# Computing the routed experts of a decoder layer on the chosen rows only, through device memory, instead of every expert on every row

## The reference

```python
x = x + attn(layernorm(x), Wqkv, Wo)            # causal, 16 heads of 16
x = x + xattn(layernorm(x), ctx, mask)          # one head of 256, softmax over 256 context rows
x = x + ffn(layernorm(x), ...)

def ffn(x):                                     # 1024 rows of 256
    probs = softmax(xf @ gate_w.T)              # 8 experts
    topk_p, topk_i = top_k(probs, 2)
    comb = (one_hot(topk_i, 8) * topk_p[..., None]).sum(axis=1)
    h = silu(einsum('nc,eic->eni', xf, w1)) * einsum('nc,eic->eni', xf, w2)    # i = 176
    y = einsum('enc,ne->nc', einsum('eni,eci->enc', h, w3), comb)
    sh = silu(xf @ sw1.T) * (xf @ sw2.T) @ sw3.T                               # width 352
    return y + sh
```

## Time and profile before

| | |
|---|---|
| median of 3 runs | 270.72 us |
| profiled execution, its span | 271.7 us |
| PE busy | 259.4 us, 95% |
| ACT busy | 174.8 us, 64% |
| DVE busy | 170.0 us, 63% |
| POOL busy | 122.4 us, 45% |
| bytes moved by DMA | 17.08 MB |

### The profile page before, as it was taken

How to read it: one execution, slowest core, us unless ns; L and a number is a source line. 1 busy time by engine, 2 the same in 40 slices (tenths; PEclk the granted TensorE clock), 3 DMA queues, 4 the chain that set the end, 5 groups by cost and what they waited for, 6 DMA issues and landing times.

```text
span 271.7 us, 4900 instructions
## 1 busy us (share of the span) xinstructions
PE 259.4 (95%) x1805; PEld 210.2 (77%) x1810; DVE 170.0 (63%) x361; ACT 174.8 (64%) x292; POOL 122.4 (45%) x133
## 2 busy tenths in 40 slices
PE   7888989999999999999989999999999999999994
PEld 2447756768877787868778888888989898888884
DVE  3675886867778666776852579638446634545453
ACT  7479379889967799888888855627565313222230
POOL 4447454988776918990954780334320000000000
PEclk9997999999999999999999999999999999999999
DMA  7891000000000000006609600000000079000002
GB/s 235 328 397 70 1 5 2 0 5 0 2 0 0 5 0 4 1 5 229 195 12 249 170 0 4 2 0 2 0 0 2 14 230 255 6 0 4 0 0 78
DMA packets 11879, 17.08 MB, mean 63 GB/s; under 512 B 1904, under 2 KB 8272, under 8 KB 11856
## 3 DMA queue, kind: packets, MB, share of 16 engines
q1 hardware_dynamic: 11856, 16.78, 19.6%
HBM read 15.63 MB, written 1.08 MB: 62 GB/s over the span
## 4 chain that ended last, share of the span: by engine, by line
PE 71%; POOL 8%; DMA 6%; DVE 6%; issue 4%; ACT 3%; SPq 2%; DVEq 0%; ACTq 0%
PE bank L789 26%; PE bank L898 13%; PE bank L802 11%; PE bank L951 4%; DMA res<-x 4%; POOL prob_lo L419 3%; DMA w_raw<-w 3%; PE bank L843 3%; PE bank L796 2%; PE bank L829 2%; PE bank L867 2%; PE bank L822 2%; PE bank L847 2%; POOL w_lo L426 1%; PE bank L824 1%
## 5 line engine op out<-in xcount | busy, mean ns | idle before, releaser
L419 POOL TENSOR_TENSOR prob_lo<-prob,prob_hi 128x1536 f16<-128x1536 f32 x16 | 49.9, 3120 | 14.9 <-ACT prob_hi L542 14.8
L789 PE MATMUL bank<-x_hi,w_hi 128*128 128x512 f32 x112 | 45.5, 406 | 0.0
L789 PE MATMUL bank<-x_hi,w_lo 128*128 128x512 f32 x112 | 44.2, 395 | 0.0
L789 PE MATMUL bank<-x_lo,w_hi 128*128 128x512 f32 x112 | 44.1, 393 | 0.0
L615 DVE TENSOR_REDUCE negm<-bank 128x2 f32<-128x512 f32 (+1 forms) x48 | 31.6, 685 | 8.6 <-PE bank L824 6.6
L771 DVE TENSOR_TENSOR h_lo<-h_c,h_hi 128x512 fp32r<-128x512 f32 x28 | 23.6, 845 | 21.0 <-ACT h_hi L581 20.8
L581 ACT CAST h_hi<-h_c 128x512 fp32r<-128x512 f32 x28 | 17.3, 617 | 24.6 <-DVE h_c L766 17.1
L757 DVE TENSOR_TENSOR h_c<-bank,h_s 128x512 f32<-128x512 f32 x28 | 19.3, 688 | 21.9 <-PE bank L789 18.3
L898 PE MATMUL bank<-w_hi,h_hi 128*128 128x256 f32 x112 | 32.9, 294 | 0.1
L575 ACT ACTIVATE h_s<-bank 128x512 f32<-128x512 f32 x28 | 16.7, 596 | 24.7 <-PE bank L789 24.7
L898 PE MATMUL bank<-w_hi,h_lo 128*128 128x256 f32 x112 | 31.6, 283 | 0.0
(11 more groups left out here) (128 smaller groups left out, 573.3 us busy)
## 6 DMA issues: line engine op xcount, KB each, us to landing
w_raw<-w SPq DMA_DIRECT2D x3, 1792.0 KB, 8.2
comb_b<-comb_dram SPq DMA_DIRECT2D x8, 256.0 KB, 4.9
res<-x SPq DMA_DIRECT2D x4, 256.0 KB, 7.0
ctxt_s<-ctx_t SPq DMA_DIRECT2D x4, 256.0 KB, 7.5
ctx_s<-ctx SPq DMA_DIRECT2D x4, 256.0 KB, 7.4
out<-res SPq DMA_DIRECT2D x8, 128.0 KB, 1.8
comb_b<-comb_dram SPq DMA_DIRECT2D x4, 224.0 KB, 4.8
wqkv_s<-wqkv SPq DMA_DIRECT2D x1, 768.0 KB, 4.8
```

The source lines that it names most:

```text
L419: eng.tensor_tensor(prob_lo[:, b % 2], prob[:, b % 2], prob_hi[:, b % 2], ALU.subtract)\
L789: ins = pe.matmul(dst, a(k), c(k), start=(k == 0 and i == 0), stop=(k == kt - 1 and i == 2))
```

## The change

The feed-forward is cut into a shared part and a routed part.

The shared part stays dense: for each batch 3 `su` steps (12 products of 256 columns; both up halves lie in one bank) and 3 `sd` steps (6 products of 256 columns), 12 of each; `sy` adds them to the residual.

The routed part works on lists. After `rk`, step `po` of each batch finds for each row and each of its two choices the position in the expert's list (products with a triangular matrix of ones), and from it a slot, 1024 slots being kept per expert. `sc` on POOL scatters the batch's normalised rows with four indirect DMAs (2 tiles x 2 choices), 258 numbers a row: 256 values, the row's number and its first expert. Before that a DMA from ACT's queue (`pad`) has written padding rows into the whole array, 8320 rows of 1032 bytes. When batch 3 is counted, `tb` on DVE works out a table of 23 tiles (16 + 7, enough for any routing): first slot, and offsets of the expert's weights. For each tile, SP reads the first slot into a register and loads 128 rows (`xg`, four buffers), PE transposes them (`tt`, which also transposes the hidden values of three tiles before), ACT and DVE split them, PE makes 6 up products of 352 columns (`ru`) with the rows stationary and the weights addressed by a register, ACT and DVE make the gated hidden values, PE makes 6 down products of 256 columns (`rd`), ACT copies the result out (three buffers), and POOL scatters it to the row's place in a second array (`ds`, `ys`). When all 23 are out, SP loads both results of each row (`yy`, eight loads of 256 KB), DVE multiplies by the gate values and adds them (`yc`, `yd`), and each of eight tiles is stored.

Comb in transposed form, its way through device memory and its multiplication go. All orders are written anew; the weights now lie in the input in the order of use, `wsh` (0.8 MB) where `w1` was loaded, `wup` (2.9 MB) where `w2` was. The cast of `wup` waits until all attention transposes are done, since its high part lies where they work.

```diff
-FT = 14
-FE = E * I // P
-SH = FT - FE
-EARLY = 3
+ST = 3
+TT = B * NT
+RT = TT * 2 + E - 1
+CAP = B * S
+PAD = E * CAP
+ROW = C + 2
+IH = I // 2
+UPC = 512
...
+        xg_dram = nc.dram_tensor("xg_dram", (PAD + P, ROW), F32, kind="Internal").ap()
+        y2_dram = nc.dram_tensor("y2_dram", (2 * B * S, C), F32, kind="Internal").ap()
...
+                elif part == "xg":
+
+                    if b == 0:
+                        sp.wait_ge(s["tab_ok"], 1)
+                        sp.wait_ge(s["sent0"], 16 * NT * 2 * 2)
+                        sp.wait_ge(s["sent1"], 16 * NT * 2 * 2)
+                        sp.wait_ge(s["o_ps"], NG * B)
+                    if b >= 4:
+                        sp.wait_ge(s["tr_ps"], b - 3)
+                        sp.wait_ge(s["dest_ok"], b - 3)
+                    row = sp.value_load(tab[0:1, 0, b:b + 1], min_val=0, max_val=PAD)
+                    sp.dma_start(xg[:, b % 4, :], xg_dram[bass.ds(row, P), :]).then_inc(s[f"xg_in{b % 4}"], 16)
...
+                elif part == "yy":
+
+                    if b == 0:
+                        for i in range(3):
+                            sp.wait_ge(s[f"y_out{i}"], 16 * len(range(i, RT, 3)))
+                    sp.dma_start(yy[:, b, :], y2_dram[2 * P * b:2 * P * (b + 1), :].rearrange("(p c) d -> p (c d)", c=2))\
+                        .then_inc(s[f"yy_in{b}"], 16)
...
+                elif part == "sc":
+
+                    if b == 0:
+                        eng.wait_ge(s["pad_out"], 16)
+                    eng.wait_ge(s["slot_ok"], b + 1)
+                    eng.wait_ge(s["pay_ok"], 2 * (b + 1))
+                    for t in range(NT):
+                        for c in range(2):
+                            eng.indirect_dma_start(xg_dram, bass.IndirectOffsetOnAxis(slot[:, NT * b + t, c:c + 1], 0),
+                                                   xrow[:, b % 2, t, :], None, bounds_check=PAD - 1, oob_is_err=False)\
+                                .then_inc(s[f"sent{b % 2}"], 16)
+                elif part == "ds":
+
+                    if b == 0:
+                        eng.wait_ge(s["tab_ok"], 1)
+                    eng.wait_ge(s[f"xg_in{b % 4}"], 16 * (b // 4 + 1))
+                    eng.tensor_scalar(dest[:, b:b + 1], xg[:, b % 4, C + 1:C + 2], t_exp[:, b:b + 1],
+                                      xg[:, b % 4, C:C + 1], ALU.is_equal, ALU.add)\
+                        .then_inc(s["dest_ok"], 1)
+                elif part == "ys":
+
+                    eng.wait_ge(s["dest_ok"], b + 1)
+                    eng.wait_ge(s["ry_ok"], b + 1)
+                    eng.indirect_dma_start(y2_dram, bass.IndirectOffsetOnAxis(dest[:, b:b + 1], 0), y_s[:, b % 3, :], None,
+                                           bounds_check=2 * B * S - 1, oob_is_err=False).then_inc(s[f"y_out{b % 3}"], 16)
...
+                elif part == "pad":
+
+                    act.wait_ge(s["pad_ok"], 1)
+                    act.dma_start(xg_dram.rearrange("(j p) c -> p j c", p=P),
+                                  pad_row[:, None, :].broadcast_to([P, PAD // P + 1, ROW])).then_inc(s["pad_out"], 16)
...
+                elif part == "tt":
+
+                    act.wait_ge(s["tr_ps"], b + 1)
+                    if b >= 2:
+                        act.wait_ge(s["ru_ps"], min(b - 1, RT))
+                    if b >= 5:
+                        act.wait_ge(s["rd_ps"], b - 4)
+                    m = moved(b)
+                    act.copy(tr_hi[:, b % 2, m], tr_ps[b % 2][:].rearrange("p (m k t) -> p m k t", m=2, k=2)[:, m])\
+                        .then_inc(s["trh_ok"], 1)
+                elif part == "ru":
+                    act.wait_ge(s["ru_ps"], b + 1)
+                    if b >= 2:
+                        act.wait_ge(s["rm_ok"], b - 1)
+                    act.activation(hr_s[:, b % 2], u_ps[b % 2][:, 0:I], ACT.Silu).then_inc(s["rs_ok"], 1)
+                elif part == "rd":
+
+                    act.wait_ge(s["rd_ps"], b + 1)
+                    if b >= 3:
+                        act.wait_ge(s[f"y_out{b % 3}"], 16 * (b // 3))
+                    act.copy(y_s[:, b % 3, :], y_ps[:, 0:C]).then_inc(s["ry_ok"], 1)
...
+                elif part == "po":
+
+                    dve.wait_ge(s["po_ps"], b + 1)
+                    link(dve.tensor_tensor(g_pos[:], pos_ps, e_base[:, None, :].broadcast_to([P, NT, E]), ALU.add))
+                    link(dve.tensor_tensor(g_prod[:, :, :, 2, :], g_oh[:],
+                                           g_pos[:, :, None, :].broadcast_to([P, NT, 2, E]), ALU.mult))
+                    link(dve.tensor_reduce(g_pick[:, b], g_prod[:], AX.X, ALU.add))
+                    dve.tensor_copy(slot[:, NT * b:NT * (b + 1), :], g_pick[:, b, :, :, 2]).then_inc(s["slot_ok"], 1)
+                    dve.tensor_copy(xrow[:, b % 2, :, C + 1], g_pick[:, b, :, 0, 1]).then_inc(s["pay_ok"], 1)
+                    dve.tensor_copy(xrow[:, b % 2, :, C], tok2[:, NT * b:NT * (b + 1)]).then_inc(s["pay_ok"], 1)
+                    if b < B - 1:
+                        if b:
+                            link(dve.tensor_tensor(cum[:, b + 1], cum[:, b], sel[:, b, 0], ALU.add))
+                            dve.tensor_tensor(cum[:, b + 1], cum[:, b + 1], sel[:, b, 1], ALU.add).then_inc(s["cum_ok"], 1)
+                        else:
+                            dve.tensor_tensor(cum[:, 1], sel[:, 0, 0], sel[:, 0, 1], ALU.add).then_inc(s["cum_ok"], 1)
...
+                elif part == "tt":
+                    dve.wait_ge(s["trh_ok"], b + 1)
+                    m = moved(b)
+                    dve.tensor_tensor(tr_lo[:, b % 2, m], tr_ps[b % 2][:].rearrange("p (m k t) -> p m k t", m=2, k=2)[:, m],
+                                      tr_hi[:, b % 2, m].bitcast(F32), ALU.subtract).then_inc(s["trl_ok"], 1)
+                elif part == "ru":
+                    dve.wait_ge(s["rs_ok"], b + 1)
+                    if b == 0:
+                        dve.wait_ge(s["hz_ok"], 1)
+                    if b >= 2:
+                        dve.wait_ge(s["tr_ps"], b + 2)
+                    dve.tensor_tensor(hr[:, b % 2, :, 0:IH], u_ps[b % 2][:, I:2 * I].rearrange("p (k i) -> p k i", k=2),
+                                      hr_s[:, b % 2].rearrange("p (k i) -> p k i", k=2), ALU.mult).then_inc(s["rm_ok"], 1)
...
+                elif part == "yc":
+
+                    if b == 0:
+                        dve.wait_ge(s["ysh_ok"], B)
+                    dve.wait_ge(s[f"yy_in{b}"], 16)
+                    dve.scalar_tensor_tensor(out=res[:, b, :], in0=yy[:, b, 0:C], scalar=g_pick[:, b // NT, b % NT, 1, 0:1],
+                                             in1=res[:, b, :], op0=ALU.mult, op1=ALU.add).then_inc(s["y1_ok"], 1)
...
+                elif part == "tt":
+
+                    if b < RT:
+                        pe.wait_ge(s[f"xg_in{b % 4}"], 16 * (b // 4 + 1))
+                    if b >= 2:
+                        pe.wait_ge(s["trl_ok"], b - 1)
+                    else:
+                        pe.wait_ge(s["on_ok"], B)
+                    if b >= 3:
+                        pe.wait_ge(s["rm_ok"], b - 2)
+                    for k in range(KC if b < RT else 0):
+                        ins = pe.transpose(tr_ps[b % 2][:, k * P:(k + 1) * P], xg[:, b % 4, k * P:(k + 1) * P], ident[:])
+                    for k in range(2 if b >= 3 else 0):
+                        ins = pe.transpose(tr_ps[b % 2][:, (2 + k) * P:(3 + k) * P], hr[:, (b - 3) % 2, k, :], ident[:])
+                    ins.then_inc(s["tr_ps"], 1)
+                elif part == "ru":
+
+                    if b % 4 == 0:
+                        n = min(4, RT - b)
+                        if b == 0:
+                            pe.wait_ge(s["tab_ok"], 1)
+                            pe.wait_ge(s["w_ok"], ST + E * KC * 2 * I // UPC)
+                        pe.load(up_regs[0:n], tab[0:1, 1, b:b + n])
+                        pe.load(down_regs[0:n], tab[0:1, 2, b:b + n])
+                        for r, regs, last in ((up_at, up_regs, KC * 2 * I), (down_at, down_regs, 2 * C)):
+                            r += [pe.snap(regs[i], min_val=0, max_val=(E - 1) * last) for i in range(n)]
+                    pe.wait_ge(s["trl_ok"], b + 1)
+                    if b >= 2:
+                        pe.wait_ge(s["rm_ok"], b - 1)
+                    for k in range(KC):
+                        for i, (a, c) in enumerate(halves(tr_hi, tr_lo, wup_hi, wup_lo)):
+                            ins = pe.matmul(u_ps[b % 2][:, 0:2 * I], a[:, b % 2, 0, k, :],
+                                            c[:, bass.ds(up_at[b] + k * 2 * I, 2 * I)],
+                                            start=(k == 0 and i == 0), stop=(k == KC - 1 and i == 2))
+                    ins.then_inc(s["ru_ps"], 1)
+                elif part == "rd":
+                    pe.wait_ge(s["trl_ok"], b + 4)
+                    if b == 0:
+                        pe.wait_ge(s["w3_ok"], 1 + E)
+                    else:
```

(6 more changed lines are left out.)

495 lines of the change are left out of this document (283 added, 212 removed).

## The result

The changed kernel takes 303.1 us (300.7 to 303.6, 4 runs) beside 270.2 us for the kernel before on the same chip: a ratio of 1.117, 95% interval 1.111 to 1.123. It is slower, as forecast, but by 33 us where the forecast had 8, and it lies 5 us above the range given.

The account below looks back on a forecast made before the run. It took TensorE to bound the feed-forward, with the relays serial: slots at 190 us, first tile at 199, 65 us of tiles to 264, and 15.4 us to the end, gave 279.4, say 280 us; range 262 to 298.

Parts of the forecast that it names:

- Stage 1: From the start to batch 3's slots, through the serial relays of batches 2 and 3: forecast at 190 us.
- Stage 2: From batch 3's slots to the first routed tile: four scatters, landing, register read and tile load, first tile at 199 us.
- Stage 3: The 23 routed tiles at 2.6 us each, plus filling and draining the pipe: 65 us, to 264.
- the floor of 2.13: TensorE's product time per routed tile, 2.13 us; a tile at this cost was named as showing the forecast wrong.
- the 0.45 us per tile: Added to each routed tile for register loads and address arithmetic on TensorE, making 2.6 us a tile.
- The row asked for: Sign of register cost in the routed tiles: idle time before TensorE's products put down to its own sequencer.
- Stage 4: From the last routed product to the end: copy, scatter, loading rows back, combining and store, 15.4 us.
- The padding write: Write of 8.6 MB from ScalarE's queue during attention, costed at nothing; a stall of up to 6 us named.
- T: Time per routed tile, taken as 2.6 us; rival of a faster kernel if under 2.1, chance 0.25.
- GpSimd was never the bound: Rival for the tile loop: scatters above 1.9 us make GpSimd pace the tiles, total 290 us, chance 0.12.
- that rival: Registers dominate TensorE's sequencer in the routed tiles: 3.2 us a tile, total 294 us, chance 0.2.
- The 0.1 given to a stage 1 that is 8 us off: Remaining chance, 0.1, that the time to batch 3's slots is 8 us off either way.

Follow-up runs that it names:

- thin kernel: Kernel before with most expert products of the feed-forward's first half left out (252 fewer; output not the reference's): 273.2 us, ratio 1.007.
- small padding write: Changed kernel with 384 instead of 1024 rows kept per expert, so the padding write is one transfer of 3.3 MB: 298.9 us, ratio 1.106.
- e13: Changed kernel with shared steps moved out of relay 3 to behind the slots, plus idle products in TensorE's waits of relays 2 and 3: 304.3 us.
- e8: Changed kernel with GpSimd's destination steps five tiles ahead and all 46 weight addresses loaded once before the first tile: 314.0 us, ratio 1.159.
- e2: Changed kernel with all remaining shared up and down steps run before the first routed tile: 302.6 us, ratio 1.122.
- e6: Changed kernel with routed weights at constant addresses, no registers on TensorE (does not compute the layer): 296.0 us.
- e9: Changed kernel with the padding write cut to 384 rows per expert and the spare rows, in four transfers: 306.9 us, ratio 1.135.
- c4: Changed kernel with destination steps ahead, next-tile address loads, idle products, 384 rows per expert, and weight splits moved ahead of relay 3: 300.1 us.
- e10: Changed kernel with all shared steps written into relay 3 moved behind the slots, no idle products: 309.3 us, ratio 1.142.
- e4: Changed kernel with some 100 idle products in TensorE's waits of relays 2 and 3: 297.2 us, ratio 1.101.

## Why the prediction was wrong in size

**What bounds the kernel before.** The text read TensorE's 95% as the bound of the feed-forward and saw that the first half was done between attention steps. It then said that "nothing shortens a relay", which held. It did not draw the other half: that the products in the waits of relays, taken with the clock that they keep up, lengthen nothing either. The thin kernel shows it, 273.2 for 270.7 us.

**Stage 1 is the step that failed, by 20 us.** It took batch 1's relay, 29.4 us, for relays 2 and 3 as well, and so, without saying it, took the length that these had before (39.9 and 34.7 us, from L687 to the ranks) to be the expert products' doing. Without most of those they took 41.4 and 37.6. In the changed kernel the 20.4 us came up in four places:

- Batch 2's attention output is normalised at 134.5 instead of 129: 5.5 us. It came at 133.0 with the small padding write, but at 132.3 to 136.3 in the six kernels with the changed kernel's code up to the slots, whole write included, so nothing of it is placed.
- Batch 2's ranks end at 168.1 instead of 158.5: 4.1 us more.
- Batch 3's attention output, ordered behind them, comes at 172.8 instead of 159: 4.2 us more. Behind the ranks stand 3.8 us to the end of batch 2's slot step, for which the sum had 1.6, and the 3 us that lighter casts were to save are not seen.
- Batch 3's relay and slot step take 37.6 us instead of 31.0: 6.6 us more. By the count from L803 to `sel` it is 35.6 against 30.1, and filled and bare it is 31.5, so 4 of these 5.5 us are the clock and the steps written into it.

The last is the part whose cause is shown. How relay 2's length divides, and what moves the attention of batches 2 and 3, was not taken apart, and stays open: with the clock mostly kept up (0.88 to 0.91 from 160 to 200 us, e13) the slots were still 15 us late. What is shown for the whole is that TensorE's products were not what held these steps up.

**Stage 2, 9 against 11.1 us.** Scatters are 1.27 us apart (forecast 1.2); the landing took 2.75, not the 1.8 of a store. The first tile's register read, issue and landing took 3.4 us (218.2 to 221.5) where the sum had 2.6, a term for which it had no row.

**Stage 3, 65 against 62.2.** The steady pace of 2.20 us is near the floor of 2.13, which the prediction itself had named as a sign of being wrong; the 0.45 us per tile were not there. The stage nearly came out by luck, since errors cancelled: the first result copy starts 8.0 us behind the first transposes, as the sum has it (1.9 + 2.6 + 3.5); the other 22 were to take 57.2 us and took 54.2, 8.8 less by the pace, but 2.5 more between the first and the second and 3.2 more in tiles 17 to 22. The row asked for, idle time put down to TensorE's sequencer, is there, six times and not at every tile. Registers cost 4 to 7 us in all, of the 10 forecast, and it was eight loads for four tiles, not the two of the text. In one place a load takes 0.34 us, 15.5 us for all 46 (e8); here part of that is hidden.

**Stage 4, 15.4 against 17.9.** The shared steps were said to lie under the scatter. They end later than it, at a clock of 0.76 (280 to 300 us): su.11 took 2.4 us instead of 1.4, and the first combining step starts 8.2 us behind the last routed product, 6.2 in e2 without them. Behind them stand 16 combining steps of 0.46 us, 7.4 us, of which the sum had counted two.

**The padding write,** costed at nothing with a stall of up to 6 us named beside it: one transfer took 6.6 us, which placed 1.3 us, and with the small write the whole is 4.2 us faster by the medians.

**The rivals.** T came near its floor in the steady tiles (2.20, not under 2.1), and the kernel is slower by 33 us: T does not decide when stage 1 is off by 20 us. GpSimd was never the bound (scatters of 1.0 us). Registers cost 4 to 7 us where that rival had some 25 (1.07 us over the floor for each of 23 tiles), at the reloads and not at each product. The 0.1 given to a stage 1 that is 8 us off was too little; the range stopped short of it.

## What to carry to other kernels

Work that fills waits can be free, and taking it away then gains nothing, here for 46 us of products (273.2 us without them, 270.7 with); before counting it as a gain, leave it out of the kernel before and time that. A chain's length measured where the clock is full holds only where something keeps it full: bare, relay 3 took 37.3 us, filled 31.5, at clocks of 0.50 and 0.88 from 180 to 200 us. A change that makes work wait for the last of a serial chain loses all overlap at once, here 93 us behind the ranks for 63, and edits at single waits gave back 8 of the 33 us.

## What the runs showed of the hardware that was not expected

- An address loaded from memory into TensorE's register takes its sequencer 0.34 us, `snap` included (46 in a row, 15.5 us, e8); the use of one, in products of 0.16 us, showed no cost in the pace (2.20 us a tile, 2.18 with constants, e6).
- A transfer of 8 or 16 KB on SP's queue took 5.8 to 7.4 us while a write of 4 to 8 MB ran on ScalarE's queue, in the chains of ten kernels, at three different places. At two of these places, with no such write running, the product behind it started 2.4 and 2.7 us after the issue.
- Of four transfers (1.0 MB three times, then 0.13 MB) issued in a row, the last two held ScalarE itself: it stood idle for 5.7 us (e9).
- VectorE's subtraction L917 took 3.28 us instead of 0.43 beside three of GpSimd's subtractions into fp32r tiles, one behind the other, and `sel` (128x16) 2.63 us (129.21) instead of 0.68 beside GpSimd's L483, which ended with it at 131.8. With the weight splits moved out of relay 3 (c4), none of its VectorE steps took over 1.3 us.
- With the relay bare, the granted clock was 0.50 over 20 us and the eight-product groups took 3.78 us (e10); with idle products in the waits 0.88 and 1.99 to 2.54 us (e13). In e4, some 100 of them in the waits of two relays made the whole 6 us faster.
